# A vision tower in slots: attention begins four slots earlier, its last three parts at three slots each, and all rounds written out

## What is computed

```python
h = window_attention(x)          # 8x8 windows, 8 heads of 8 channels, rotary q and k, softmax, projection
n = layernorm(h)
h = h + (mamba(n) + n)           # rmsnorm, in-projection, conv of 4 taps, silu, delta = softplus(.),
                                 # scan h_t = exp(delta*A)*h_{t-1} + delta*x*B over an image's 4096
                                 # positions, 128 channels x 16 states; y = (h.C + x*D) * silu(z), out-projection
h = h + experts(layernorm(h))    # router, top 2 of 6 experts, each 64 -> 64 -> 64 -> 64 with relu
```

## Time and profile before

| | us |
|---|---|
| median of three runs | 1921.03 |
| lowest, highest | 1919.44, 1929.98 |
| the profiled execution | 1921.91 |
| its span | 1920.1 |
| TensorE busy | 1396.5 |
| VectorE busy | 1341.6 |
| GpSimd busy | 1209.0 |
| ScalarE busy | 1086.1 |
| start of the first scan | 207.9 |

### The profile page before, as it was taken

The page is one execution under the profiler, slowest core; times in us unless marked ns, Lnnn a source line. Parts: engine busy times, 40 slices in busy tenths (PEclk is TensorE's granted clock), DMA queues, the critical chain, the costliest instruction groups (busy, mean ns, idle before and its releaser), DMA issues. The chain is left out here.

```text
span 1920.1 us, 31423 instructions
## 1 busy us (share of the span) xinstructions
PE 1396.5 (73%) x8148; PEld 648.9 (34%) x8148; DVE 1341.6 (70%) x1835; ACT 1086.1 (57%) x2020; POOL 1209.0 (63%) x1665
## 2 busy tenths in 40 slices
PE   3765768787969697786869687686868687666565
PEld 1443434343425243243424333242424333121111
DVE  1111688888786857878686867879686877878941
ACT  1234657675565747575475756566575857564432
POOL 2014486867685856767585765768586776967651
PEclk9877979796878878797788878796987978676755
DMA  2001686666565655666465665566566666777820
GB/s 63 1 14 57 162 226 192 195 187 173 159 200 156 182 167 157 189 186 173 138 185 174 165 190 162 174 169 193 150 170 184 172 198 175 213 192 204 222 70 6
DMA packets 214770, 304.52 MB, mean 159 GB/s; under 512 B 78924, under 2 KB 79128, under 8 KB 214424
## 3 DMA queue, kind: packets, MB, share of 16 engines
q1 hardware_dynamic: 214552, 302.09, 55.8%
HBM read 274.75 MB, written 20.97 MB: 154 GB/s over the span
## 5 line engine op out<-in xcount | busy, mean ns | idle before, releaser
L1262 POOL TENSOR_TENSOR hc<-hs,c_rep 128x512 f32<-128x512 f32 x512 | 652.2, 1274 | 461.0 <-DVE hs L1014 458.6
L1014 DVE TENSOR_TENSOR_SCAN hs<-bank,state,xd 128x512 f32<-128x512 f32 x512 | 650.8, 1273 | 83.2 <-issue 57.8
L767 ACT ACTIVATE bank<-dl,a_neg 128x512 f32<-128x512 f32 x512 | 350.3, 687 | 209.7 <-DVE hs L1014 186.7
L1005 DVE TENSOR_TENSOR xd<-xd,bank 128x512 f32<-128x512 f32 x512 | 337.1, 663 | 57.1 <-PE bank L439 53.3
L1032 DVE TENSOR_REDUCE neg_max<-bank 128x8 f32<-128x512 f32 x128 | 88.1, 688 | 281.1 <-PE bank L528 272.6
L538 PE MATMUL bank<-q_diag,k_heads 128*128 128x128 f32 x1024 | 226.4, 348 | 6.0 <-ACT shift L760 4.5
L538 PEld LDWEIGHTS bank<-q_diag,k_heads 128*128 128x128 f32 x1024 | 193.8, 229 | 82.8 <-issue 65.5
L775 ACT ACTIVATE probsT<-bank 128x512 f32<-128x512 f32 x128 | 76.4, 597 | 256.1 <-PE bank L539 255.6
L528 PE MATMUL bank<-k_heads,q_diag 128*128 128x512 f32 x256 | 175.1, 772 | 56.3 <-DMA q_diag<-rot 25.5
L449 PE MATMUL bank<-hc,wts 128*32 128x512 f32 x1024 | 182.8, 777 | 4.0 <-POOL hc L1262 2.6
L1334 POOL TENSOR_TENSOR ew<-ew,e 128x512 f32<-128x512 f32 x96 | 121.4, 1264 | 64.9 <-ACT e L760 64.8
(11 more groups left out here) (176 smaller groups left out, 2493.3 us busy)
## 6 DMA issues: line engine op xcount, KB each, us to landing
xd<-xdel_rows SPq DMA_DIRECT2D x512, 256.0 KB, 4.1
dl<-delta_rows SPq DMA_DIRECT2D x512, 256.0 KB, 3.8
delta_rows<-delta SPq DMA_DIRECT2D x16, 512.0 KB, 6.3
xdel_rows<-xdel SPq DMA_DIRECT2D x16, 512.0 KB, 3.1
xin<-in_x_dram SPq DMA_DIRECT2D x32, 128.0 KB, 2.4
q_diag<-rot SPq DMA_DIRECT2D x32, 128.0 KB
out_dram<-res SPq DMA_DIRECT2D x256, 16.0 KB
k_heads<-rot SPq DMA_DIRECT2D x128, 16.0 KB
```

Of the source, the lines that this page charges most:

```text
L767: act.activation(decay_ps[n % 2][:, :], dl[:, n % 4, :], ACT.Exp, scale=a_neg[:, g:g + 1])\
L1005: dve.tensor_tensor(xd[:, n % 8, :], xd[:, n % 8, :], b_ps[:, :], ALU.mult).then_inc(injected.sem, 1)
L1014: dve.tensor_tensor_scan(hs[:, n % 4, :], decay_ps[n % 2][:, :], xd[:, n % 8, :], state[:, g:g + 1], ALU.mult, ALU.add).then_inc(scanned.s ...
L1262: pool.tensor_tensor(hc[:, n % 8, :], hs[:, n % 4, :], c_rep[:, BAND * h:BAND * h + BAND], ALU.mult)\
```

## The change

1. `attention_at` puts s = 0 into slot 5, so the step s of attention is in slot s + 5 of its round, and 27 to 31 are in slots 0 to 4 of the next.
2. The table `AT` gives parts 0 to 4 two slots each and parts 5 to 7 three. For parts 5 to 7 the maximum comes one slot behind S.
3. The sums on GpSimd come at s = 5, the k2 and q2 products on VectorE at s = 4, `k_heads` at s = 6 and 7; the k and q matmuls move from `attend_first` to `attend`. `rec` and `att` come at s = 30 (slot 3), the turn of `att` at 31 (slot 4), and the projection is a step of its own in slot 5, right behind T and P.
4. SP loads x in slot 1, copies heads and queries in slots 10 and 11.
5. All steps of the first norm come three slots earlier. `h_ln` is made in slot 17 of the norm's own round, with three buffers in place of two; the wait in front of it asks for the chunk three before.
6. `outT` is the memory of `fT`.
7. All rounds are written out.
8. The small matmuls of 8 columns in front of `keys_queries` and `layer2` (L466, L694) are left out.

```diff
-AT = {"S": [9 + 2 * _w for _w in range(NW)], "max": [11 + 2 * _w for _w in range(NW)],
-      "T": [12 + 2 * _w for _w in range(NW)], "P": [13 + 2 * _w for _w in range(NW)]}
+AT = {"S": [9, 11, 13, 15, 17, 20, 23, 26], "max": [11, 13, 15, 17, 19, 21, 24, 27],
+      "T": [12, 14, 16, 18, 20, 23, 26, 29], "P": [13, 15, 17, 19, 21, 24, 27, 30]}
...
-        h_ln = sb("h_ln", [128, 2, NW, C])
+        h_ln = sb("h_ln", [128, 3, NW, C])
...
-        outT = sb("outT", [128, 512])
+
+        outT = fT
...
-            return (c + 3, n - 9) if n >= 9 else (c + 2, n + 23)
+            return (c + 3, n - 5) if n >= 5 else (c + 2, n + 27)
...
-            for c in range(-3, 3):
-                body(c, c % 2)
-            with eng.Fori(3, NCH - 4, 2) as c:
-                body(c, 1)
-                body(c + 1, 0)
-            for c in range(NCH - 3, NCH + 2):
+            for c in range(-3, NCH + 2):
                 body(c, c % 2)
...
-                        if n == 4:
+                        if n == 1:
                             load(c + 3)
-                        if 13 <= n < 15:
-                            heads(c + 3, 4 * (n - 13), 4 * (n - 12))
-                        if n == 14:
+                        if 10 <= n < 12:
+                            heads(c + 3, 4 * (n - 10), 4 * (n - 9))
+                        if n == 11:
                             queries(c + 3)
...
-
-                pe.matmul(uses[0].bank[0:32, 0:8], col("y_sel", 0, 32), xT[:, 0:8], start=True, stop=True)
...
             def attend_first(k, s):
+                if s in AT["T"]:
+                    turned(k, AT["T"].index(s))
+                if s in AT["P"]:
+                    values(k, AT["P"].index(s))
+
+            def attend(k, s):
                 if s == 1:
                     keys_queries(k, ("k", "q"), ("wk", "wq"))
                 if s == 3:
                     keys_queries(k, ("k2", "q2"), ("wk2", "wq2"))
...
-                if s == 30:
+                if s == 31:
                     use = A["oT"]
...
+            def project(k):
+                use = A["proj"]
+                fill(use, k)
+                pe.wait_ge(A["oT"].drained, A["oT"].empty(k))
...
-
-                pe.matmul(uses[0].bank[0:32, 0:8], col("y_sel", 0, 32), e1[:, 0, 0:8], start=True, stop=True)
...
                         attend_first(k, s)
+                    if has(c + 2) and n == 5:
+                        project(c + 2)
...
-                if s in (5, 6):
-                    for h in (2 * s - 10, 2 * s - 9):
+                if s in (6, 7):
+                    for h in (2 * s - 12, 2 * s - 11):
...
-                if s == 29:
+                if s == 30:
                     dve.wait_ge(A["P7"].drained, A["P7"].empty(k))
...
-                if n == 9:
+                if n == 6:
                     use = A["proj"]
                     dve.wait_ge(use.filled, use.full(k))
...
+                if n == 17:
+                    if past(k - 3):
+                        pool.wait_ge(F["mo"].drained, F["mo"].empty(k - 3))
+                    pool.tensor_tensor(h_ln[:, k % 3, :, :], hid[:, :, :], lnx[:, :, :], ALU.add).then_inc(ln1_pool.sem, 1)
```

More of the change, by code:

```diff
@@ L267, in past @@
         def past(k):
-            return not isinstance(k, int) or k >= 0
+            return k >= 0
         def group(n):
@@ L275, in has @@
         def has(k):
-            return not isinstance(k, int) or 0 <= k < NCH
+            return 0 <= k < NCH
         def ahead(c, n, k):
@@ L511, in attend @@
                     last.then_inc(use.filled, 1)
-                if s == 31:
-                    use = A["proj"]
-                    fill(use, k)
-                    pe.wait_ge(A["oT"].drained, A["oT"].empty(k))
-                    for i in range(4):
-                        last = pe.matmul(use.bank[:, 128 * i:128 * i + 128], attT[:, 128 * i:128 * i + 128], col("wp"),
-                                         start=True, stop=True)
-                    last.then_inc(use.filled, 1)
+            def project(k):
+                use = A["proj"]
+                fill(use, k)
+                pe.wait_ge(A["oT"].drained, A["oT"].empty(k))
+                for i in range(4):
+                    last = pe.matmul(use.bank[:, 128 * i:128 * i + 128], attT[:, 128 * i:128 * i + 128], col("wp"),
+                                     start=True, stop=True)
+                last.then_inc(use.filled, 1)
             def scores(k, w):
@@ L1089, in experts @@
                     dve.wait_ge(ln1_pool.sem, ln1_pool.at(k, 15))
[L1090 removed]
+                    dve.tensor_tensor(h1[:, :, :], use.bank[:, :].rearrange("p (w h) -> p w h", w=NW), h_ln[:, k % 3, :, :], ALU.add)\
                        .then_inc(use.drained, 1)
```

40 lines of the change are left out of this document (17 added, 23 removed).

## The result

| | before | after |
|---|---|---|
| median, us | 1923.7 (1919.4 to 1930.0, 4 runs) | 2035.9 (2032.0 to 2041.4, 4 runs) |
| ratio, 95% interval | 1 | 1.0583 [1.0538, 1.0627] |
| profiled execution (span), us | 1921.9 (1920.1) | 2032.0 (2029.8) |
| granted clock, share of full | 0.806 | 0.792 |

The change makes the kernel 5.8% slower. The medians are of all executions, while the ratios leave out those more than 1.5% over the fastest of their kernel, so a ratio is not the quotient of its two medians. The forecast was 1938 us, with a range of 1872 to 1982: the direction of its likeliest case was right and the size was not. The direction is not much to its credit, since the prediction gave "slower" only 0.51 of its chances, and none of its cases was priced above 1973.

What follows compares the result with a forecast made beforehand. No engine was full: TensorE held slots 0 to 3 and 20 on, VectorE 15 to 19. Profiled 1921.9 + 32.4 (12 rounds at +2.7) + 4 (outer rounds) + 1 (start) - 21.1 (jumps) = 1938 us; range 1872 to 1982.

Steps and rivals of the forecast that it cites:

- The jumps: Four jumps back of the two-round Fori, each costing 4.9 to 6.1 us before scan 4; writing out saves 21.1 us.
- Slots 20 to 3: Slot 20 to slot 3 of the next round: TensorE's lighter load, partly returned by waits; -2.0 us a round.
- relief of 6.2 us: TensorE in slots 20 to 3 loses two each of T, P and S, 2 x 3.1 us a round.
- the walk: Slot-by-slot tracing of engine queues in slots 20 to 3: waits behind one-slot maxima return 6 to 7 us.
- Slots 4 to 9: Att transposes and projection move to slots 4 and 5, delaying conv1 and silu: +2.5 us a round, bounds 0 and 3.9.
- Slots 10 to 14: ScalarE gets v copies, k_heads, square and roots, and loses x's copy: +1.2 us a round, bounds 0 and 1.7.
- 15 to 20: Added attention pieces fit TensorE's idle time; VectorE gets two more maxima: +1.0 us a round, bounds -1.5 and +2.5.
- The start and the outer rounds: One more part of attention before the first scan, +1 us; rounds 0 and 13 together, +4 us.
- (3): Rival for slots 20 to 3: waits return everything, +0.9 in place of -2.0 a round; 1973 us, chance 0.22.
- (1): Rival: TensorE keeps its relief from slot 20 to 3, -6.2 in place of -2.0; 1888 us, chance 0.27.
- (2): Rival: denser slots 15 to 19 raise the clock from slot 20 on, saving 41 us; 1897 us, chance 0.07.
- The silu some 3 us later: Sign in the profile after: each round's silu comes some 3 us later behind scan 4.

Runs made afterwards that it cites:

- e1: The kernel before with only its rounds written out (no Fori jumps): 1901.1 against 1925.3 us, ratio 0.9903.
- e2: The kernel after with the old table AT (two slots per part, maxima two slots behind scores), attention still from slot 5: 1953.2 against 1925.3 us, ratio 1.0189.
- e3: The kernel after with the scores of parts 5 to 7 one slot earlier, so all maxima come two slots behind: 1948.5 against 1925.3 us, ratio 1.0173.
- e5: The kernel after with S5 to S7 issued right behind T and P in their slots, maxima still one slot behind: 1966.3 against 1926.3 us, ratio 1.0257.
- e11: The kernel after with useless matmuls in slots 13 (two), 15 (three) and 24 (two): 2058.2 against 1918.4 us, ratio 1.0736.
- experiment 6: e3 with the projection behind conv1 and x's turn in slot 5, and x's copy behind conv1's on ScalarE: 1971.0 against 1926.3 us, ratio 1.0279.
- e7: e1 without the two small matmuls of 8 columns (L466, L694): 1905.0 against 1926.3 us, ratio 0.9904.
- e10: e1 with useless 128 x 512 matmuls at the end of slots 15 (two), 17 (three) and 19 (two): 1859.1 against 1927.5 us, ratio 0.9641.
- e12: e1 with useless matmuls at the end of slots 13 (two), 15, 17 and 19 (three each): median 1862.2 against 1918.4 us, ratio 0.9488.
- experiment 9: The kernel of experiment 6 with useless 128 x 512 matmuls at the end of slots 13 (two) and 15 (three): 1922.8 against 1927.5 us, ratio 0.9981.

## Why the prediction was right or wrong

**The jumps: right.** Taken at 21.1 us; experiment 1 measured 24 on the median, and the four stretches behind a jump, of which the earlier trace rows has two, exceed the others by 21.0. The Trainium skill (Advanced Engine Details and Errata, Control Flow Timing) gives a compare-and-branch about 108 ns, by which writing out four jumps saves an estimated 0.4 us; the runs differ and decide for the long jump. That the reason is the loading of instructions, as the Trainium skill (Runtime: NRT & Kernel Launch, Instruction fetch mechanics) has it, fits but no run here isolates it.

**Slots 20 to 3: the step that failed.** The term was −2.0 us a round, with bounds of −6.2 and +0.9. Measured, from e1 to after: (11.66 + 45.85) − (9.74 + 43.11) = **+4.7**. The term was a relief of 6.2 us less a return of 4.2. The windows tell the two apart: over slots 20 to 3 of rounds 2 to 12 TensorE is busy 48.5 us and idle 4.4 in e1, busy 47.2 and idle 10.3 after. So the idle time grew by 6.0, and the busy time fell by 1.3 only.

The return is what the walk had found, 6 to 7 us. I then took 4.2 because "some expert work will slide into the gaps". It did not. The queues are in order and each wait stops the next engine's whole queue: the 7.45, 5.68 and 3.43 us that VectorE waits are waits with everything behind them. From the end of S5 to the next weight matmul it is 3.9 us (1446.75 to 1450.65), where the walk had about 4. Experiments 2, 3 and 5 show that the maxima one slot behind scores that stand last are the cause of the larger part of the loss.

The relief of 6.2 us is the larger miss, 4.9 of the 6.7 us, and it has two parts. One is a miscount that the tables `AT` show: slots 20 to 3 lose two S and two T, but no P. They hold seven P before and seven after (112 matmuls of that line in e1 and in after, while those of S go from 14 to 10 and those of T's first line from 64 to 48). By the earlier trace rows two S and two T are 5.1 us. The other is the clock: the walk and its bound were those of full clock. While TensorE is busy in slots 20 to 3, the share is 0.79 in e1 and 0.74 after; it is 0.50 in the piece of slot 25 shown above. In e3 and e5, which have the same pieces at other places, it is 0.84 and 0.85, and TensorE is busy 41.9 and 41.1 us. Busy time times that share is 38.2 in e1 and 35.0 to 35.1 in all of after, e2, e3 and e5: these four do the same work, less than e1's, and after does it slowest. In e3 and e5 the relief is real: (10.16 + 38.18) and (10.18 + 38.09) against 52.85 in e1, −4.5 and −4.6 a round. With the count put right the walk's upper bound is +2.0, and e11, which meets slots 25 and 0 to 3 at 1.00 (the stretch from slot 20 at 0.77, with two matmuls more in slot 24), measured +2.3. What took the clock down in the kernel after is not shown.

One wait was named and given no number: `rec` in the same slot as P7, with scan 4 behind it. Slot 3 grew from 2.4 to 4.8 us, more than the whole +1.9 of scans 0 to 4:

```profile
1363.76 0.55 DVE L1045 RECIPROCAL rec<-pv 128x64 f32<-128x64 f32 x1 [1.71 <-ACT pv L753]
```

In e3 and e11, where the clock in slots 0 to 3 is at 1.00, the slot takes 3.4 us.

**Slots 4 to 9: right in kind, by another path in part.** +2.5 predicted, +1.7 measured after and +2.9 in e2. Conv1 waits for the projection and that for the copy, as expected. TensorE's timeline of the next round after:

```profile
1484.68 1.13 PE L510 MATMUL bank<-wts,xT 128*128 128x128 f32 x8 [0.78 <-ACT xT L753]
...
1486.74 1.13 PE L565 MATMUL bank<-xnT,conv_w 128*128 128x512 f32 x2
...
1490.54 1.20 PE L575 MATMUL bank<-xnT,z_w 64*128 64x512 f32 x4 [1.27 <-ACT xz L837]
```

Taking the projection out of that place gave 1.6 us of it back (experiment 6). But the silu, by which the term was reckoned, starts 15.1 us behind scan 4 where it starts 14.3 behind it in e1, and not some 3 later. What holds the scans is slot 7 (7.4 us for 2.5), where VectorE waits for the k matmul, which stands behind the same pieces, with scan 8 in its queue:

```profile
1376.85 1.41 DVE L1036 SCALAR_TENSOR_TENSOR rot<-bank,wts 128x512 f32<-128x512 f32 x2 [3.62 <-PE bank L463]
```

**Slots 10 to 14 and 15 to 20: within their bounds after, not in e2.** +1.2 predicted, +0.7 measured (ScalarE is busy 12.59 of 14.20 us in the window); +1.0 predicted, +1.4 measured after, which is what the two maxima add to VectorE's busy time (21.6 to 23.0 us); +2.7 in e2, over the upper bound of 2.5. How much of the first is due to the v and k_heads copies, and what the third h_ln does, was not tried alone. The small matmuls were put at nothing, and no run shows that they are anything (experiment 7). The prediction read from one pair of unlike router steps that GpSimd matters here. The sixteen runs of the second (L1134) in the kernel before bear it out: with no GpSimd step beside it, it takes 0.21 us, and in eleven of them, where a GpSimd step of 1.27 us had begun up to 0.14 us earlier or begins with it, it takes 1.20 to 1.33 us and ends 0.06 or 0.07 us behind that step. In e1 it takes 0.21 to 0.25 us in most rounds. VectorE's busy time in scans 15 to 20 is 22.5 us before and 21.6 in e1, which is 0.9 of the 1.6 us by which they are shorter there.

**The start and the outer rounds: too small.** The first scan starts at 218.0 us after and at 207.9 before: +10 where +1 was taken. But that time is 199.9 in e1, 210.4 in e7 and 213.1 in e10, which have the same order there (e7 without its small matmuls), so most of the 10 us cannot be put down to the change. Round 0 takes 95.1 us for 86.1 in e1 and round 13 takes 91.2 for 87.6: 12.6 together, where 4 was taken. Round 0 loses 5.8 of its 9.0 us from scan 20 on; round 13 loses nothing there, but some 2 us each in scans 0 to 4 and 15 to 20.

**The sum.** Between the spans of e1 and after lie 131.5 us: 101.5 in rounds 1 to 12 (8.5 each, 2.7 predicted, so 32.4), 12.6 in rounds 0 and 13, 18 up to the first scan. Of the 69 us by which rounds 1 to 12 are off, the term from slot 20 to 3 carries 12 × 6.7 = 80, and the two terms that came out smaller than taken give some back. Against the forecast that makes, with 9 us in the outer rounds and 17 up to the first scan, the 94 us by which the profiled execution lies over 1938.

**The rivals.** (3), the lockstep takes all, has the right mechanism: it had 1973 because its price was the walk's +0.9, with the relief of 6.2 in it. (1) did not happen. For (2), the clock: slots 15 to 19 are at a mean share of 0.90 for 0.72, as the rival wanted, but from scan 20 on it is 0.74 where it was 0.79 before (and 0.74 in e1 as well), so nothing came of it there; that the new gaps did this was only argued. The observation behind it, that nearly the same work takes 36 or 45 us with the clock, turned out to be the largest saving in this kernel (experiments 10 and 12), by another edit than this one.

Of what the prediction said would show it: TensorE under 85% from slot 20 on, the waits of the weight matmul, scans 0 to 4 the same in every round (at 11.7, though, not 10), slots 10 to 14 held by ScalarE, and slots 15 to 19 within 1.5 us of 25 came true. The silu some 3 us later did not.

## What to carry to other kernels

Where several in-order engines hand work round slot by slot, the distance between a producer and its consumer is to be counted from the producer's place in its slot's queue: a consumer one slot behind a piece that is queued last stops every queue behind it, and moving three such pieces cost more here than the removed load could give. When a walk through the queues says that a relief is given back, take the walk's number. Count the relief as carefully as the return, piece by piece from the tables of before and after, and let the upper bound hold the slower clock as well. And look for stretches where TensorE is half idle in front of one where it is the bound: what it does there can raise the clock with which it enters (experiment 10). It does not always do so: after, slots 15 to 19 are at 0.90, and the stretch behind them is at 0.74.

## What the runs showed of the hardware

**Work of no use can pay.** In the kernel before the stretch from scan 20, TensorE's own, ran at a mean share of 0.79, and in e1 at 0.74. Seven matmuls of 512 columns a round in the idle slots ahead of it lifted e1's to 0.88, and took its 1901 us to 1859 (e10, 0.9641 of the kernel before); with eleven, three of seven times give 0.9488 and the others are no better than with seven. The windows of experiment 10 show the extremes, 34.7 us at 1.00 and 44.6 at 0.69 for nearly the same matmuls; the means are 38.46 and 43.11. The Trainium skill (TensorE: Matmul & The Clock Gate, Loop structure matters more than you think) says that dense matmuls keep the clock and long waits lose it; experiment 10 agrees, with those numbers.

**A local saving may be lost to the clock.** Experiment 6 took 1.6 us out of a stretch where TensorE waits, and the total rose by 22 us while the clock of the run fell from 0.806 to 0.769; experiment 9 gave 48 us back with nothing but more matmuls. That the clock made all of the 22 us, and that the 22 us are more than noise, is not shown.

**It has a limit.** Where a wait is part of the bound, the clock gives back only its own part: slot 25 of the kernel after takes 9.9 us at 0.68 and still 7.2 at 1.00, and experiment 11, which has it at 1.00 in rounds 2 to 12, is no faster. And the rounds of e3 and e12 take 34.5 and 42.5, or 34.7 and 42.1 us in turn for the same work; what decides between the two was not found.

**A small VectorE step can take as long as the GpSimd step beside it.** L1134 of the kernel before (128 x 48 elements) takes 0.21 us alone and up to 1.33 us beside a GpSimd step of 1.27 us, and ends just behind it. By where such steps fall, VectorE is busy 22.5 or 21.6 us in scans 15 to 20 of two kernels (before, e1) that have the same work there.
